# A normalisation folded into scaled weights: the first attention of a two-layer adaLN block

## The reference

```python
def _layernorm(x, axis=-1, eps=1e-05):
    m = jnp.mean(x, axis=axis, keepdims=True)
    v = jnp.var(x, axis=axis, keepdims=True)
    return (x - m) / jnp.sqrt(v + eps)
...
mod = (_silu(L0_c) @ L0_wmod).reshape(L0_c.shape[0], 6, 1, -1)
sa, ca, ga, sb, cb, gb = (mod[:, 0], mod[:, 1], mod[:, 2], mod[:, 3], mod[:, 4], mod[:, 5])
...
h = _layernorm(x, axis=-1) * (1 + ca) + sa
x = x + ga * _L0_attn_ref(h, ...)      # Wq (512 x 16 x 32), Wk, Wv (512 x 16)
h = _layernorm(x, axis=-1) * (1 + cb) + sb
x = x + gb * _L0_ffn_ref(h, ...)
```

## Time and profile before

| | |
|---|---|
| three executions | 1808.51, 1811.09, 1811.34 us, median 1811.09 |
| the profiled execution | 1810.07 us |
| its span | 1808.2 us, 28904 instructions |
| TensorE busy over the span | 98% |
| VectorE, ScalarE, GpSimd busy | 70%, 61%, 24% |
| the span's chain, by engine | TensorE 95%, VectorE 3%, ScalarE 1%, DMA 1%, issue 1% |

### The profile page before, as it was taken

One profiled execution on the slowest core, in us unless ns is written; L12 is line 12 of the kernel. 1 busy time (PEld: TensorE's weight loads), 2 busy tenths in 40 slices (PEclk: granted clock), 3 DMA queues, 4 the chain that ended last, 5 costly groups with the idle time before them and its releaser, 6 DMA issues.

```text
span 1808.2 us, 28904 instructions
## 1 busy us (share of the span) xinstructions
PE 1778.4 (98%) x8799; PEld 1483.5 (82%) x8799; DVE 1269.1 (70%) x2977; ACT 1096.2 (61%) x2648; POOL 438.3 (24%) x431
## 2 busy tenths in 40 slices
PE   6998999999999999999999999999999999999999
PEld 4666888888888888888888888888888878888887
DVE  5897787887777677766677777777777777454532
ACT  6665766666666666766667676666666664342331
POOL 2234404041323324041612123140413132011000
PEclk9899999999999999999999999999999999999999
DMA  9026667677676867687776867676777878213110
GB/s 350 7 82 233 187 186 219 203 203 217 180 226 179 224 194 201 188 264 206 223 219 194 236 184 223 200 217 195 220 218 204 235 193 271 90 45 116 40 31 24
DMA packets 239367, 331.24 MB, mean 183 GB/s; under 512 B 26008, under 2 KB 165528, under 8 KB 238880
## 3 DMA queue, kind: packets, MB, share of 16 engines
q1 hardware_dynamic: 238736, 328.93, 61.2%
q10 hardware_dynamic: 528, 1.05, 0.1%
HBM read 200.39 MB, written 129.50 MB: 182 GB/s over the span
## 4 chain that ended last, share of the span: by engine, by line
PE 95%; DVE 3%; ACT 1%; DMA 1%; issue 1%; POOL 0%; SPq 0%; DVEq 0%; ACTq 0%; POOLq 0%
PE ps L2132 28%; PE ps L2202 19%; PE ps L2185 12%; PE ps L2325 11%; PE ps L2168 10%; PE ps L2310 5%; PE ps L1257 2%; PE ps L2165 1%; PE ps L120 1%; PE ps L1165 1%; PE ps L1172 1%; DMA wm<-in_L_wmod_dram 1%; PE ps L1224 1%; PE ps L1233 0%; PE ps L2374 0%
## 5 line engine op out<-in xcount | busy, mean ns | idle before, releaser
L2132 PE MATMUL ps<-hA,wq 128*128 128x512 f32 x1536 | 378.3, 395 | 0.0
L2202 PE MATMUL ps<-wo,oT 128*128 128x512 f32 x1536 | 366.3, 389 | 0.2 <-DVE acc L2754 0.2
L2202 PEld LDWEIGHTS ps<-wo,oT 128*128 128x128 f32 x1536 | 288.1, 188 | 60.1 <-issue 0.4
L2479 ACT ACTIVATE pt<-pd 128x1280 fp32r<-128x1280 f32 x128 | 162.9, 1273 | 273.4 <-PE ps L2185 237.0
L2132 PEld LDWEIGHTS ps<-hA,wq 128*128 128x128 f32 x1536 | 279.5, 188 | 53.7
L2710 DVE CUSTOM_DVE_ANT_0 ps<-ps,mask 128x384 f32<-128x384 f32 (+7 forms) x512 | 220.6, 484 | 143.7 <-PE ps L2168 139.6
L2461 ACT ACTIVATE probs<-ps,nmax 128x384 f32<-128x384 f32 (+7 forms) x512 | 250.2, 503 | 61.6 <-DVE nmax L2710 59.1
L2469 ACT ACTIVATE probs<-probs,rinv 128x384 f32<-128x384 f32 (+7 forms) x512 | 232.6, 526 | 47.8 <-DVE rinv L2721 47.8
L2730 DVE STREAM_TRANSPOSE tp<-probs 128x384 f32<-128x384 f32 (+3 forms) x512 | 215.4, 478 | 4.4 <-ACT probs L2469 4.4
L2185 PE MATMUL ps<-pt,V 128*128 128x256 f32 (+1 forms) x896 | 216.4, 329 | 1.5 <-DVE oT L2743 0.4
L2738 DVE TENSOR_TENSOR pd<-pd,pt 128x1280 fp32r<-128x1280 f32 x128 | 193.3, 1510 | 2.6 <-ACT pt L2479 2.6
(11 more groups left out here) (268 smaller groups left out, 2739.6 us busy)
## 6 DMA issues: line engine op xcount, KB each, us to landing
turned_blocks<-tp SPq DMA_DIRECT2D x128, 640.0 KB, 3.4
pd<-turned_blocks SPq DMA_DIRECT2D x512, 160.0 KB, 3.5
wq_next<-in_L_attn_w_q_dram SPq DMA_DIRECT2D x16, 1024.0 KB, 7.1
wo_in<-in_L_attn_w_o_dram SPq DMA_DIRECT2D x15, 1024.0 KB, 9.7
turned_weights<-hf_chunk SPq DMA_DIRECT2D x168, 64.0 KB, 2.8
wm<-in_L_wmod_dram SPq DMA_DIRECT2D x4, 2048.0 KB, 15.6
turned_values<-tv SPq DMA_DIRECT2D x32, 256.0 KB, 4.0
xh_m<-turned_weights SPq DMA_DIRECT2D x28, 256.0 KB, 3.8
```

The source lines that it names most:

```text
L2132: last = nc.tensor.matmul(ps[:, bank, :], w[i][:, c, cols], hT[k][:, c, b * S:(b + 1) * S], start=(c == 0 and n == 0), stop=(c == DC - 1 a ...
L2202: last = nc.tensor.matmul(ps[:, bank, :], oT[x_][:, b, h, AT[r] * P:(AT[r] + 1) * P], wo[y_][:, h, :], start=(h == 0 and n == 0), stop=(h ...
L2479: nc.scalar.activation(flat(pt[:]), flat(pd[:, u % 2].bitcast(F32)), ACT.Copy).then_inc(phi_done, 1)
```

## The change

It rests on this: with r = 1/std and mean m of a row, (r (x - m)(1 + ca) + sa) W + b = r (x W' - m sum(W')) + (sa W + b), with W' = (1 + ca) W. So:

- TensorE turns the raw rows X, as soon as they are loaded. `columns_of` copies them out of PSUM as they are.
- VectorE makes four scaled copies of the weights, `wscaled`, one for each batch (`scale_weights`). Column 48 of them is 1/D in each of the 512 rows, so `columns1` gives the row's mean beside q, k and v.
- `sum_weights` (TensorE) makes the negative column sums of W' in the places of that column, `fold` (VectorE) adds them to `same_half`; `project` with the sum, `folds`, adds the halves and subtracts the mean's part at once.
- `offsets` (TensorE) makes sa W for each batch, with sa, spread over 128 columns, as the stationary operand; `add_bias` (VectorE) adds the bias. `products` then multiplies by r and adds the offset, one instruction for each of the four row tiles.
- `normal1`, `shift` and the tile `xh1` in this role are gone.
- wmod's first four vectors arrive one by one, CA first, ahead of X of batch 0; SA comes after Wq, Wk and Wv; the loads and the numbering in `MODS` follow. `wq_in` lies elsewhere in SBUF.
- The calls on ScalarE, VectorE and TensorE are put in a new order. Batch 0 has its scaling, sums and offsets by itself, batches 1 to 3 together, after the matmuls of the fourth vector.

The diff, with plain renamings, waits and constants of places further on left out:

```diff
@@ -253,6 +253,12 @@
...
+    QKV = 3 * E0
+    with ExitStack() as early:
+        wscaled = sb(early, "wscaled", [P, B, DC, P // 2], F32)
+        folds = sb(early, "folds", [P, B, QKV], F32)
+        offs = sb(early, "offs", [P, B, QKV], F32)
+        pick_sums = sb(early, "pick_sums", [P, P], F32)
@@ -308,7 +314,7 @@
...
-    MODS = [(layer, v) for layer in range(2) for v in range(6)]
+    MODS = [(0, MOD_CA), (0, MOD_SA)] + [(0, v) for v in range(MOD_GA, 6)] + [(1, v) for v in range(6)]
@@ -381,22 +391,30 @@
...
+        def load_one(m):
+            which = MODS[m][1]
+            sp.dma_start(wms[m // 2][:, :, m % 2 * D:(m % 2 + 1) * D],
+                         wmod0.rearrange("(c p) n -> p c n", p=P)[:, :, which * D:(which + 1) * D]) \
+                .then_inc(mod_loaded(m)[0], 16)
         def load_x(b):
...
+        load_one(0)
...
-        load_wm(0)
...
-        load_x(1)
+        load_one(1)
...
-        load_wm(1)
+        load_x(1)
+        load_one(2)
...
+        load_one(3)
@@ -439,6 +457,11 @@
...
+    def mod_loaded(m):
+        return {0: (ld_wm[0], 16), 1: (ld_b, 64), 2: (ld_wm[1], 16), 3: (ld_at_first, 48)} \
+            .get(m, (ld_wm[m // 2 % NSLOT], 16 * (m // 2 // NSLOT + 1)))
@@ -471,6 +494,9 @@
...
+        nc.gpsimd.memset(wscaled[:, :, :, QKV:QKV + 1], 1.0 / D).then_inc(consts, 1)
+        nc.gpsimd.memset(wscaled[:, :, :, QKV + 1:], 0.0).then_inc(consts, 1)
+        nc.gpsimd.memset(pick_sums[:, QKV::HALF], -1.0).then_inc(consts, 1)
@@ -568,24 +594,13 @@
...
-        def normal1(b):
-            act.wait_ge(inv1, b + 1)
+        def columns_of(b, chunks=range(DC)):
...
-                act.wait_ge(turned, chunk(1, b - 1, DC - 1) + 1)
-            for t in range(TB * b, TB * (b + 1)):
-                last = nc.scalar.activation(xh1[:, t % TB, :], rows(X, t), ACT.Identity, bias=shift[:, t:t + 1],
-                                            scale=rstd1[:, t:t + 1])
-            last.then_inc(xh1_done, 1)
-        def modulated1(b, chunks=range(DC)):
-            if b == 0:
-                act.wait_ge(mods_done, 1)
-            else:
...
-                modulate(hT1[:, c, :], bank_of(k), 0, MOD_CA, MOD_SA, c, b).then_inc(taken, 1)
+                nc.scalar.activation(hT1[:, c, :], ps[:, bank_of(k), :], ACT.Copy).then_inc(taken, 1)
@@ -658,49 +673,41 @@
...
             nc.scalar.activation(bias_p[0:1, :], bias_r[0:1, :], ACT.Copy).then_inc(bias_step, 1)
+        copy_mod(0)
+        take_mod(0)
         root1(0)
-        normal1(0)
-        copy_mod(0)
+        columns_of(0)
         copy_mod(1)
-        take_mod(0)
+        copy_columns1(0)
         take_mod(1)
-        act.wait_ge(wcat_done, 2)
-        modulated1(0)
+        columns_of(1)
+        copy_mod(2)
+        take_mod(2)
+        copy_columns1(1)
+        copy_mod(3)
+        exponentials(0)
+        take_mod(3)
         root1(1)
-        copy_columns1(0)
-        normal1(1)
-        copy_mod(2)
-        copy_mod(3)
-        modulated1(1, range(1))
-        take_mod(2)
-        modulated1(1, range(1, 3))
-        take_mod(3)
-        modulated1(1, range(3, 4))
-        exponentials(0)
         copy_rows(0)
-        copy_columns1(1)
         copy_weights(0)
-        root1(2)
         copy_weights(1)
         copy_centroids()
...
         copy_weights(3)
         copy_o(0)
-        normal1(2)
         copy_mod(4)
         round_bias()
-        modulated1(2, range(1))
+        columns_of(2, range(1))
         take_mod(4)
         copy_rows(1)
         root2(0)
+        root1(2)
         copy_mod(5)
-        root1(3)
-        exponentials(1)
-        modulated1(2, range(1, 3))
-        take_mod(5)
         copy_rows(2)
         copy_rows(3)
-        modulated1(2, range(3, 4))
+        exponentials(1)
+        take_mod(5)
+        columns_of(2, range(1, 4))
         whole(0, range(1))
         copy_mod(6)
@@ -712,15 +719,15 @@
...
         rounded(0, range(2, 3))
-        normal1(3)
         rounded(0, range(3, 4))
         take_mod(7)
-        modulated1(3, range(3))
+        columns_of(3, range(3))
+        root1(3)
         exponentials(2)
...
         drain(0)
-        modulated1(3, range(3, 4))
+        columns_of(3, range(3, 4))
         copy_rows(5)
@@ -895,8 +902,6 @@
...
-            nc.vector.scalar_tensor_tensor(shift[:, v], mv1[:, v, 0], -1.0, rstd1[:, v], ALU.mult, ALU.mult) \
-                .then_inc(inv1, 1)
@@ -926,8 +931,11 @@
         def products(b):
...
-            link(nc.vector.tensor_tensor(qkv[:], pv, bcat[:].rearrange("p (o k) -> p o k", o=1)
-                                         .to_broadcast([P, TB, 3 * E0]), ALU.add))
+            for t in range(TB):
+                last = nc.vector.scalar_tensor_tensor(qkv[:, t, :], pv[:, t, :], rstd1[:, TB * b + t:TB * b + t + 1],
+                                                      offs[:, b, :], ALU.mult, ALU.add)
+            last.then_inc(folded, 1)
+            dve.wait_ge(folded, QKV_FIRST if b == 0 else FOLD_REST + b)
@@ -999,8 +1007,31 @@
...
+        def scale_weights(batches):
+            for b in batches:
+                col = mod[0][:, DC * MOD_CA:DC * MOD_CA + DC, b:b + 1].to_broadcast([P, DC, QKV])
+                last = nc.vector.scalar_tensor_tensor(wscaled[:, b, :, 0:QKV], col, 1.0, wcat[:, :, 0:QKV], ALU.add, ALU.mult)
+            last.then_inc(wcat_done, 1)
+        def spread_over(v, batches):
+            return v.rearrange("p (o k) -> p o k", o=1).to_broadcast([P, len(batches), QKV])
+        def fold(batches, sums):
+            dve.wait_ge(first_step, sums)
+            v = slice(batches[0], batches[-1] + 1)
+            nc.vector.tensor_tensor(folds[:, v, :], sums_bank[:, v, :], spread_over(same_half[:, 0:QKV], batches), ALU.add) \
+                .then_inc(folded, 1)
+        def add_bias(batches, made):
+            dve.wait_ge(first_step, made)
+            v = slice(batches[0], batches[-1] + 1)
+            link(nc.vector.tensor_tensor(offs[:, v, :], offs_bank[:, v, :], spread_over(bcat[:], batches), ALU.add))
         def sum_bias():
-            dve.wait_ge(ld_b, 48)
+            dve.wait_ge(ld_b, 64)
@@ -1020,32 +1051,40 @@
         constant_rows()
         statistics1(0)
+        sum_queries()
+        dve.wait_ge(mods_sb, 1)
+        dve.wait_ge(wcat_done, WCAT_SUMMED)
+        scale_weights(range(1))
+        scale_weights(range(1, B))
+        dve.sem_inc(mods_done, 1)
         inverse1(0)
-        sum_queries()
-        mods(2, 0, MOD_SA, MOD_GA)
-        statistics1(1)
         sum_bias()
-        inverse1(1)
+        fold(range(1), SUMS_FIRST)
+        add_bias(range(1), OFFS_FIRST)
         scores(0)
         mods(3, 0, MOD_GA, MOD_SB)
-        statistics1(2)
+        add_bias(range(1, B), OFFS_REST)
+        fold(range(1, B), SUMS_REST)
+        statistics1(1)
         outputs(0)
-        inverse1(2)
+        inverse1(1)
         products(1)
         add_outputs(0, range(2))
         shifted()
         add_outputs(0, range(2, 4))
         statistics2(0)
-        statistics1(3)
+        statistics1(2)
         normal2(0)
         low_bias()
         mods(6, 0, MOD_SB, 6)
         outputs(1)
-        inverse1(3)
+        inverse1(2)
         one_hot()
+        statistics1(3)
         add_outputs(1)
         scores(2)
         statistics2(1)
+        inverse1(3)
         outputs(2)
         normal2(1)
         scores(3)
@@ -1175,16 +1214,16 @@
     def first_tensor(pe):
...
-        pe.wait_ge(ct_step, SILU_DONE)
+        pe.wait_ge(first_step, SILU_DONE)
...
-        last.then_inc(ct_step, 1)
+        last.then_inc(first_step, 1)
         def turn(kind, b, chunks=range(DC)):
-            src, ready = {1: (xh1, xh1_done), 2: (xh2, xh2_done)}[kind]
-            pe.wait_ge(ready, b + 1)
+            src = {1: X[b], 2: xh2}[kind]
+            pe.wait_ge(*{1: (ld_x[b], 16), 2: (xh2_done, b + 1)}[kind])
@@ -1196,19 +1235,40 @@
         def columns1(b):
+            pe.wait_ge(wcat_done, WCAT_FIRST if b == 0 else WCAT_SCALED)
+            pe.wait_ge(consts, CONSTS)
...
-                pe.wait_ge(logits, b)
+                pe.wait_ge(folded, QKV_FIRST if b == 1 else FOLD_REST + b - 1)
...
-                last = nc.tensor.matmul(ps[at:at + HALF, BANK_P, :], wcat[:, c, :], hT1[:, c, :], start=(c < 2), stop=(c >= 2))
+                last = nc.tensor.matmul(ps[at:at + HALF, BANK_P, :], wscaled[:, b, c, :], hT1[:, c, :], start=(c < 2), stop=(c >= 2))
...
+        def sum_weights(batches):
+            pe.wait_ge(wcat_done, WCAT_FIRST if batches[0] == 0 else WCAT_SCALED)
+            pe.wait_ge(consts, CONSTS)
+            v = slice(batches[0], batches[-1] + 1)
+            for c in range(DC):
+                last = nc.tensor.matmul(sums_bank[:, v, :], pick_sums[:], wscaled[:, v, c, 0:QKV], start=(c == 0), stop=(c == DC - 1))
+            last.then_inc(first_step, 1)
+        def offsets(batches):
+            pe.wait_ge(mods_sb, 2)
+            for b in batches:
+                for c in range(DC):
```

(31 more changed lines are left out.)

30 lines of the change are left out of this document (17 added, 13 removed).

## The result

The changed kernel takes 1818.92 us in the median (1816.45 to 1820.41), the kernel before, on the same chip, 1810.79 (1808.51 to 1811.34). The ratio is 1.005, with a 95% interval of 1.0036 to 1.0064: slower by 8 to 9 us, in the forecast's direction and inside its range, 3 us above its number. The profiled execution took 1818.92 us, with a span of 1817.2 against 1808.2.

The account below looks back on a forecast made before the run. TensorE is busy from 50 us to the end, so front delays to its queue move the end. Terms -2.7, +6.1, -0.5, +0.9, +1.2 sum to +5.0: 1815.1 us against the profiled 1810.07 (median 1816.0); range 1810 to 1821.

Parts of the forecast that it names:

- VectorE's wait for the offsets, with fold and statistics: Ahead of outputs(0): VectorE idles 4 us for OFFS_REST, then does the adds and statistics1(1); +6.1 us.
- shift, qkv in four: VectorE behind outputs(0): shift (0.82) goes, qkv takes four instructions for one (0.3 more taken); net -0.5 us.
- Point 1: Opening: project(0) ends earlier, at 24.9 instead of 27.6, without ScalarE's normalisation and one megabyte in front; -2.7 us.
- rival (a): Opening: TensorE's clock already rises in the transposes, project(0) ends at 22.9, sum +3.0, 1814.1 us; chance 0.25.
- Point 2: First add onto X comes later, 48.5 instead of 45.6, as outputs(0) queues on VectorE behind the wait for offsets; +2.9.
- No transfer is late for it: Loads ahead of the offsets cost nothing: GA lands at 21.8, SB about 27, wanted at 27 and 31.
- The small terms: VectorE and TensorE: shift gone (0.82), four qkv instructions (0.3), batch 0's sums, offsets and project at 1.1 each.
- Point 3: columns1(2), 63.1 before: root1(2) and gate rows stand ahead of ScalarE's column copies; +0.9 on top, +3.8 in total there.
- Point 4: Around 80 us: root1(3) brings two table loads ahead of exponentials(2), delaying the dense gates; +1.2 us, 0 to 2.8.
- (c): 28 to 77 us: ScalarE, not VectorE and the offsets, sets the pace, so the kernel gets faster, 1804; chance 0.09.
- (d): 45 to 55.3 us: part of the delay is made up where TensorE ran at the lower clock, 1813.4; chance 0.07.
- (b): TensorE's clock stays low through the offsets, +3.8 there and up to +2 in the opening; 1819 to 1821; chance 0.14.

Follow-up runs that it names:

- own semaphore: Changed kernel, with SB's transfer counted on its own semaphore, so make_mod(3) doesn't wait for centroids and dense weights; 1816.77 us, ratio 1.0031.
- statistics into the wait: Changed kernel, with VectorE's statistics1(1) moved ahead of add_bias and fold of batches 1 to 3; 1814.02 us, ratio 1.0024.
- roots together: Changed kernel, with root1(3) right behind root2(1) and inverse1(3) behind normal2(1), so two table loads go; 1817.83 us, ratio 1.004.
- more work on ScalarE: Changed kernel, with four extra copies of X's last batch on ScalarE where normal1(3) stood; 1819.46 us, ratio 1.0051.
- delay in before: Kernel before, with batch 2's row moments taken two times more on VectorE (4.97 us) ahead of outputs(0); 1814.28 us, ratio 1.0029.
- order of before: Changed kernel, with SB's own semaphore and VectorE's statistics, ScalarE's roots and copies nearly in the old kernel's order; 1811.16 us, ratio 1.0003.
- outputs(0) into the wait: Changed kernel, with exponentials(0) earlier on ScalarE and outputs(0) ahead of the offsets of batches 1 to 3 on VectorE; 1817.36 us, ratio 1.0037.
- turn_o(0) ahead: Order of before, plus mods(3) and outputs(0) between statistics1(1) and (2), turn_o(0) ahead of project(1), copy_o(0) ahead of gate rows; 1810.21 us, ratio 1.0011.
- four moves: Changed kernel, with own semaphore, earlier statistics1(1), roots together, and exponentials(1) and two batch-2 column copies earlier on ScalarE; 1813.5 us, ratio 1.0015.

## Why the prediction was right, and where its sizes were off

All profiles together say where the time is set (one profiled execution each; start of each place in us, project(0) by its end):

| | project(0) ends | outputs(0) | third dense_gates | span | between |
|---|---|---|---|---|---|
| before | 27.6 | 36.36 | 81.28 | 1808.2 | 1726.9 |
| changed | 23.4 | 41.85 | 90.29 | 1817.2 | 1726.9 |
| own semaphore | 24.9 | 39.49 | 88.06 | 1814.6 | 1726.5 |
| statistics into the wait | 25.4 | 37.85 | 85.38 | 1812.1 | 1726.7 |
| roots together | 26.5 | 42.13 | 89.25 | 1816.1 | 1726.9 |
| more work on ScalarE | 24.0 | 40.72 | 90.49 | 1817.7 | 1727.2 |
| delay in before | 24.6 | 37.63 | 84.75 | 1811.8 | 1727.1 |
| order of before | 26.7 | 41.83 | 85.97 | 1813.1 | 1727.1 |
| outputs(0) into the wait | 26.0 | 34.27 | 86.22 | 1812.8 | 1726.6 |
| turn_o(0) ahead | 23.3 | 31.95 | 78.73 | 1805.6 | 1726.9 |

In all thirteen profiles the time from the third dense_gates to the end lies between 1726.5 and 1727.5 us, while the dense gates move by 11.8. So all that differs between these executions is made in the first 80 us. What a change of this stage is worth can be read at 80 us, and all of it counts. That was the forecast's first sentence on what bounds the kernel, and the delay in the kernel before bears it out without the change.

The forecast's sum against the trace, in us (the wait is from the end of project(0) to outputs(0): 8.7 before, 18.4 after):

| | forecast | measured |
|---|---|---|
| project(0) | -2.7 | -4.2 |
| VectorE's wait for the offsets, with fold and statistics | +6.1 | +9.7 |
| shift, qkv in four | -0.5 | 0.0 |
| columns1(2) | +0.9 | +2.5 |
| two table loads | +1.2 | +1.0 |
| sum | +5.0 | +9.0 |

**Point 1: right in direction, rival (a) in its size, and part of the size is chance.** The 16 opening transposes took 3.65 us, still the lower rate; make_mod(1) behind them ran at the upper one (8 records in 1.06), and project(0) ended at 23.4, near that rival's 22.9. (The clock column of the profile reads 1.00 all through both openings, beside rows at half rate, so the level there is read from the rows' lengths.) make_mod(1) waited for `(ld_b, 64)`, so for bq, bk and bv behind SA's transfer too, and began at 16.79, where the forecast had it start with SA at 15.8; SA had landed at 15.7 (6.17 + 9.5). Rival (a) took 2 us off the sum for the early clock, and that was wrong: TensorE reached make_mod(3) earlier and stood there for w_in. In the runs with the same semaphore and a slower opening (project(0) at 24.0, 25.4 and 26.5) TensorE reached make_mod(3) at 32.3 to 33.7 and stood for nothing, and the offsets' add came at 37.2 to 38.6, as in the changed kernel's (38.29). The gain at the front was cut off by a transfer that doesn't move.

The opening ends anywhere from 23.3 to 26.7 us in the eleven profiles of the changed code, with the place where the clock rises; "TensorE: Matmul & The Clock Gate" of the Trainium skill, Part 1, says that the moment differs from run to run, and these traces agree. It does so in the kernel before as well: 27.6 in the one profile that the forecast had, 24.6 in the run with the delay, whose code is the same up to there. Of the -4.2 some 3 us may be the execution's and not the change's.

**Point 2: the mechanism was right, the term that was mis-sized is the wait, by the step "No transfer is late for it".** The wait that the forecast put at 4 us was 7.61. The forecast costed SB's own transfer (27.6, as it said) and not the semaphore, which counts the centroids and w_in too. That is 2.2 us of standing and, with the clock that fell after it, 1.0 in the sums and 0.4 in the offsets: 3.6, all of the 9.7 - 6.1. With a semaphore of its own the offsets ended 11.0 after project(0), as summed. This 3.6 can't be added to the loss by itself: it fell to an execution whose opening was 1.5 us faster than forecast, and in the slower ones just named it was nothing. The first two terms together were forecast at +3.4 and came to +5.5. That VectorE's order made a loss is shown by the one move of the statistics (1.0024 for 1.005, clear of each other). The order of before with the own semaphore leaves 1.0003; how the rest of the 9 us divides among the semaphore, the roots and ScalarE's order isn't shown, since those runs differ by less than their intervals.

**The small terms.** The four instructions of qkv took 0.79 us, for 0.34, +0.45 where 0.3 was taken. The shift's going saved 0.75 us between outputs(0) and qkv, about as forecast. But the products behind qkv (L940) took 1.60 us, where L932 had taken 1.31, both beside GpSimd's work (with GpSimd idle, at 24.38, L940 took 1.23), and that took the rest: -0.75 + 0.45 + 0.3 is nothing. For batches 1 to 3 fold and add_bias took 0.31 each, and the sums, offsets and project of batch 0 1.06 to 1.07, as forecast.

**Point 3: the order was read rightly, the clock was left out.** From the first add to columns1(2) it was 2.5 us more than before, for 0.9. ScalarE's part is the smaller one: the forecast let copy_mod(5) run at once behind the root, and it waited 0.73 us more for make_mod(5), whose 8 records took 1.94 us at the lower clock; still, from the root to TensorE's release it was 5.5 us for 5.2. The larger part is TensorE's own. From its release at 67.12 to columns1(2) it took 4.0 us where the forecast had 2.8 and the kernel before 3.0: the clock fell again with the wait of 1.86 us (0.61 from 66 to 69), and make_mod(7) took 1.55 for 1.06. With ScalarE's order changed (four moves) the stretch from the first add to columns1(2) is 17.7, as before. Why the clock stays low from 48 to 63 us isn't shown. The new matmuls aren't needed for it: in the kernel before with the delay it was 0.50 from 45 to 57 us, and columns1(2) came 3.8 later for a first add 1.8 later. Nor is the delay enough: in the run with the order of before outputs(0) came as late as in the changed kernel, and the clock was 1.00 from 48 to 57.

**Point 4: right.** 1.0 for 1.2, with the stall of 1.17 at the predicted place; without the loads the stretch to the third dense_gates was 1.4 shorter.

**The rivals.** (c) falls by its own condition: it needed the offsets within 7.2 us of project(0), and they came after 14.8, with VectorE standing for 7.6. (d), a loss made up at the lower clock, falls for the changed kernel: the clock took more there, not less. (b), a lower clock in the offsets, is what partly happened, for 1.4 us and after a gap: with no gap ahead of them the same matmuls ran at the upper level (1.00 from 30 to 36 us).
